# Row moments of the first layernorm taken on ScalarE with accumulators, in four of five pairs of tiles, in a graph-network kernel

## The chip, the cores and the metric

One core of one Trainium2 chip runs the whole program. The metric is device time in microseconds (us) of one execution; the times of a kernel are given as the median of several runs. Engines are named as the profile names them: PE is TensorE's matmuls and PEld its weight loads, DVE is VectorE, ACT is ScalarE, POOL is GpSimd, SP is SyncE; a q behind a name is that engine's DMA issuing.

## What is computed

Two graph networks in a row on 1250 nodes of 1024 features and 20000 edges. Only the head of the first one matters here:

```python
def layernorm(x, g, b):
    m = jnp.mean(x, axis=-1, keepdims=True)
    v = jnp.mean((x - m) ** 2, axis=-1, keepdims=True)
    return (x - m) * jax.lax.rsqrt(v + LN_EPS) * g + b

h = layernorm(x, ln_in_g, ln_in_b)          # x: 1250 x 1024
h = jax.nn.relu(h @ W1 + b1)                # 1024 -> 512
h = h @ W2 + b2                             # 512 -> 256
for i in range(3):                          # message passing, 20000 edges
    agg = jax.ops.segment_sum(h[src], dst, num_segments=n)
    ...
```

After it come a decoder back to 1024 features, two more layernorms, and two neighbourhood layers with 1024x1024 weights.

## The kernel before

The program has four stages, one after the other: `graph_block` (the first 168 us), the encoder, the decoder, and the two neighbourhood layers. The change touches only the first.

`graph_block` does two things at once. It turns the edge list into a dense matrix of edge counts (visits: VectorE builds two one-hot masks with `is_equal` at lines 410 and 411, PE multiplies them at line 586 into five banks), and it computes relu(layernorm(x) @ W1 + b1) (`dense`, line 622). The 1250 nodes are 10 tiles of 125 rows, taken as 5 pairs p = 0 to 4; the tiles of a pair are u = 0 and 1. A pair also has 5 groups j of 7 visits: six each at first, then the body of `more`, and one more each at the end.

Every engine's program is written out by hand and runs in that order; semaphores are the only link. For one pair the path of the layernorm is this. SP loads the rows into `x_rows[u]`, of which there are only two: the load of tile (p+1, u) may start once `normalize(p, u)` has read (p, u). VectorE's `statistics(p)` takes the moments with two `bn_stats` for each tile (line 386), two `bn_aggr` (394) and one add (396); ScalarE takes the root (`take_root`, 240); VectorE's `normalizer(p)` makes the reciprocal with a Newton step and the shift (63 to 71, 402). ScalarE's `normalize(p, u)` writes `xhat[u]` (248), PE turns it (`turn_norm(p, u)`, 579), ScalarE applies gain and bias and rounds (`affine(p, u)`, 257 and 262), VectorE keeps the rest (`norm_low`, 442), and PE can multiply.

On PE, the loop of pair p runs the four column blocks `dense(p-1, 0..3)` between the groups of counts of pair p; `turn_norm(p, 1)` stands behind `dense(p-1, 3)` and `turn_norm(p+1, 0)` at the loop's end. The turned rows go to banks that hold the products of `dense(p-1, 1)` and `dense(p-1, 2)`, so `turn_norm(p, 1)` also waits until ScalarE's `relu(p-1, 2)` (line 282) has read them, and `dense(p-1, 3)` waits for `relu(p-1, 0)`. VectorE writes its masks into a ring of 12 places and so can be two groups ahead of PE. ScalarE's other work is `read_counts` (274, ten copies out of the banks), `z1_high` (291) and the rounding of the weights (267).

In VectorE's program `statistics(1)` stands in pair 0 behind the visits of group 2; `statistics(p+2)` stands at the end of pair p, ahead of `z1_low(p-1)` and the visits of the next pair. `normalizer(p+1)` stands behind group 0 of pair p.

Of the kernel before, what the change touches and what calls it, by code (L numbers as in the profile page):

```python
# [5 lines left out]
ALU = mybir.AluOpType  # L6
ACT = mybir.ActivationFunctionType
AX = mybir.AxisListType
F32 = mybir.dt.float32
# [6 lines left out]
D, H, B, LAYERS = 1024, 512, 256, 3  # L16
NT = 125
# [3 lines left out]
PAIRS = T // 2  # L21
# [4 lines left out]
EPS = 1e-5  # L26
# [81 lines left out]
def graph_block(nc, block, sem, io, s):  # L108
# [20 lines left out]
    z1_mm, z1_relu, z1_hi, z1_split = sem("z1_mm"), sem("z1_relu"), sem("z1_hi"), sem("z1_split")  # L129
    at_stored, eye_added = [sem("at_stored0"), sem("at_stored1")], sem("eye_added")  # L130
    padded, places_set = sem("padded"), sem("places_set")

    at = Map(nc, s.work_at)
    w1 = at("w1", [128, 2, KD, H], F32R)
# [23 lines left out]
    var_eps, root, rstd, shift, scratch = [at(n, [128, 2], F32) for n in ("var_eps", "root", "rstd", "shift", "scratch")]  # L158
    trips_i = at("trips_i", [128, PAIRS], I32)
    iota = at("iota", [128, KEYS], F16)  # L160
    assert at.at <= nc.sbuf_usable_end, at.at - nc.sbuf_usable_end

    at = Map(nc, s.wide_at)
# [73 lines left out]
    def _(act):  # L237
        def take_root(p):
            act.wait_ge(var_ready, p + 1)
            act.activation(root[0:NT, :], var_eps[0:NT, :], ACT.Sqrt).then_inc(root_ready, 1)  # L240

        def normalize(p, u):
            t = 2 * p + u
            act.wait_ge(norm_ready, p + 1)
            act.wait_ge(x_in[u], 16 * (p + 1))
            if p > 0:
                act.wait_ge(xhat_read, t - 1)
            act.activation(xhat[u][0:NT, :], x_rows[u][0:NT, :], ACT.Identity, bias=shift[0:NT, u:u + 1],
                           scale=rstd[0:NT, u:u + 1]).then_inc(xhat_ready, 1)

# [54 lines left out]
        for n in range(2, KD // 2):  # L305
            w1_high(n)
        affine(0, 1)
        take_root(1)
        normalize(1, 0)
        normalize(1, 1)  # L310
        w1_high(KD // 2)
        for p in range(1, PAIRS):
            read_counts(p - 1)
            if p + 1 < PAIRS:
                take_root(p + 1)
            affine(p, 0)
            relu(p - 1, 0)
            relu(p - 1, 1)
            if p + 1 < PAIRS:
                normalize(p + 1, 0)  # L320
            relu(p - 1, 2)
            relu(p - 1, 3)
            z1_high(p - 1)
            affine(p, 1)
            if p + 1 < PAIRS:
                normalize(p + 1, 1)
# [55 lines left out]
    def _(dve):  # L382
# [2 lines left out]
            for h in range(2):  # L385
                dve.bn_stats(stats[0:NT, u, h, :], x_rows[u][0:NT, 512 * h:512 * h + 512]).then_inc(stat_step, 1)

        def statistics(p):
            if p > 0:
                row_sums(p, 0)  # L390
                row_sums(p, 1)
            dve.wait_ge(stat_step, 6 * p + 4)
            for u in range(2):
                dve.bn_aggr(mean_var[0:NT, u, :], stats[0:NT, u, :, :]).then_inc(stat_step, 1)
            dve.wait_ge(stat_step, 6 * p + 6)
            dve.tensor_scalar(var_eps[0:NT, :], mean_var[0:NT, :, 1], EPS, None, ALU.add).then_inc(var_ready, 1)

        def normalizer(p):
            dve.wait_ge(var_ready, p + 1)
            dve.wait_ge(root_ready, p + 1)  # L400
            newton_rstd(dve, norm_step, 5 * p, rstd[0:NT, :], var_eps[0:NT, :], root[0:NT, :], scratch[0:NT, :])
            dve.scalar_tensor_tensor(out=shift[0:NT, :], in0=mean_var[0:NT, :, 0], scalar=-1.0, in1=rstd[0:NT, :],
                                     op0=ALU.mult, op1=ALU.mult).then_inc(norm_ready, 1)

        def visit(n, g, v):

# [107 lines left out]
            dve.tensor_scalar(pick[0:EP, j, :], spread, table[0:EP, j:j + 1], None, ALU.is_equal).then_inc(picked, 1)  # L514
        dve.tensor_copy(visits[0:EP, :], spread.rearrange("p (g v) -> p g v", v=VISITS)[:, :, STATIC]).then_inc(row_step, 1)
        dve.tensor_copy(chunk_ids[0:EP, :], table[0:EP, 0:2]).then_inc(row_step, 1)
        statistics(0)
        w1_low(0)
        normalizer(0)
        dve.wait_ge(picks, 1)  # L520
# [7 lines left out]
        for p in range(PAIRS):  # L528
            for j in range(GROUP):
                for v in range(STATIC - 1):  # L530
                    visit(n, GROUP * p + j, v)
                    n += 1
                if p == 0:
                    if j == 1:
                        w1_low(1)
                        norm_low(0, 0)
                    if j == 2:
                        statistics(1)
                        w1_low(2)
                        w1_low(3)  # L540
                    if j == 3:
                        norm_low(0, 1)
                        normalizer(1)
                else:
                    if j == 0 and p + 1 < PAIRS:
                        normalizer(p + 1)
                    if j == 2:
                        norm_low(p, 0)
            if p == 0:
                dve.wait_ge(trips_known, PAIRS + 1)  # L550
            if p > 0:
                dve.wait_ge(hot_free, GROUP * STATIC * p + GROUP)
            last_trip = dve.value_load(trips_i[0:1, p:p + 1], min_val=p + 2, max_val=(C - STATIC) * (p + 1) + 1)
            more(p, first_trip, last_trip)
            first_trip = last_trip
            for j in range(GROUP):
                visit(n, GROUP * p + j, STATIC - 1)
                n += 1
            if p > 0:
                norm_low(p, 1)  # L560
            if p + 2 < PAIRS:
                statistics(p + 2)
            if p == 0:
                w1_low(KD // 2)
            else:
                z1_low(p - 1)
# [1342 lines left out]
```

## Time and profile before

| | us |
|---|---|
| median of 3 runs | 1071.99 |
| lowest, highest | 1071.13, 1073.99 |
| the profiled execution | 1074.08 |
| its span in the profile | 1072.3 |
| first stage, until PE's last `dense` | 168 |

So 1.8 us of the profiled execution lie outside its span, and it took 2.1 us more than the median. All starts of instructions below count from the start of the span. A profile row gives the start, the time (of all instructions of the row together, first start to last end), engine, line, operation, output and input, and in brackets the idle time ahead of it and what ended that idle time. Neighbouring rows overlap by some 0.1 us, because an instruction's end is drained while the next one starts; so the cost of a piece of a queue is best read as the distance between two starts.

### The profile page before, as it was taken

The numbers are of one execution on the slowest core, as the hardware profiler recorded it, in microseconds if no ns is written. First come the engines' busy times: TensorE is split into PE (matmuls) and PEld (weight loads), VectorE is DVE, ScalarE is ACT, GpSimd is POOL, SyncE is SP. The second block draws the span as 40 slices with busy tenths as digits, with TensorE's granted clock in tenths as the row PEclk, the third lists the DMA queues.
The fourth block names the chain that finished last, engine by engine and source line by source line (L and its number), as shares of the span: only waits on it lengthen the run. The fifth ranks groups of instructions, "written<-read, shape, count | busy, mean of one in ns | idle before, by whom it ended". The sixth has DMA issues, their size and how long they took to land.

```text
span 1072.3 us, 14807 instructions
## 1 busy us (share of the span) xinstructions
PE 1002.2 (93%) x4862; PEld 812.9 (76%) x4862; DVE 536.6 (50%) x1314; ACT 351.5 (33%) x632; POOL 263.8 (25%) x320
## 2 busy tenths in 40 slices
PE   4779899989897898999999999999999999999996
PEld 2367678878787687887777777778887777877774
DVE  7978974374658887333223332222234333334545
ACT  5545552152526477321111221113341011222221
POOL 3000003741416330735004324005206003300000
PEclk9698999999998999999999999999999999999999
DMA  9296344893003584414223104243325335103444
GB/s 327 67 220 186 49 64 89 195 204 84 2 20 109 188 281 150 144 32 138 100 100 102 45 20 160 67 141 128 108 87 166 120 97 164 46 1 121 154 133 133
DMA packets 48263, 127.13 MB, mean 119 GB/s; under 512 B 17775, under 2 KB 18784, under 8 KB 48016
## 3 DMA queue, kind: packets, MB, share of 16 engines
q1 hardware_dynamic: 33622, 74.91, 23.8%
q0 software_dynamic: 8288, 37.29, 12.9%
q10 hardware_dynamic: 6298, 14.21, 3.9%
q8 instruction: 33, 0.54, 0.2%
q14 instruction: 22, 0.18, 0.1%
HBM read 101.76 MB, written 45.13 MB: 137 GB/s over the span
## 4 chain that ended last, share of the span: by engine, by line
PE 83%; DVE 7%; ACT 3%; issue 3%; DMA 2%; POOL 1%; SPq 0%; ACTq 0%; DVEq 0%; POOLq 0%
PE bank L1724 42%; PE bank L1745 17%; PE bank L622 5%; PE bank L1071 5%; PE bank L1103 4%; PE bank L1431 4%; PE bank L586 3%; DMA x_rows<-x 1%; DVE wide L957 1%; PE bank L1412 1%; DVE wide L959 1%; PE bank L1445 1%; ACT xt_f L257 1%; DMA w_f<-W_pairs 1%; PE bank L579 0%
## 5 line engine op out<-in xcount | busy, mean ns | idle before, releaser
L1665 DVE TENSOR_TENSOR h_stage<-h_turned,h_stage 128x1000 fp32r<-128x1000 f32 x80 | 105.5, 1320 | 370.2 <-ACT h_stage L1597 370.2
L1724 PE MATMUL bank<-w_neigh,h_stage 128*125 128x512 f32 x960 | 227.2, 397 | 3.4 <-issue 3.4
L1724 PE MATMUL bank<-w_self,h_stage 128*125 128x512 f32 x960 | 230.3, 395 | 0.0
L1724 PEld LDWEIGHTS bank<-w_neigh,h_stage 128*125 128x125 f32 x960 | 178.2, 187 | 47.3 <-issue 3.6
L1724 PEld LDWEIGHTS bank<-w_self,h_stage 128*125 128x125 f32 x960 | 178.0, 186 | 45.6
L1745 PE MATMUL bank<-g_rows,a_stage 125*125 125x512 f32 x800 | 192.4, 395 | 0.0
L1597 ACT ACTIVATE h_stage<-h_turned 128x1000 fp32r (+1 forms) x80 | 83.8, 1049 | 305.9 <-PE bank L1724 293.5
L1745 PEld LDWEIGHTS bank<-g_rows,a_stage 125*125 125x125 f32 x800 | 148.4, 186 | 37.4
L1562 POOL CAST w_self<-w_stage 128x512 fp32r<-128x512 f32 x32 | 22.7, 711 | 230.2 <-PE bank L1724 221.9
L1103 PE MATMUL bank<-a_turned,gn 125*128 125x418 f32 x360 | 70.5, 354 | 2.8 <-DVE gn L963 2.8
L1103 PEld LDWEIGHTS bank<-a_turned,gn 125*128 125x128 f32 x360 | 67.0, 188 | 4.2 <-DVE gn L963 3.4
L622 PE MATMUL bank<-xt,w 128*128 128x252 f32 x480 | 65.0, 294 | 0.7 <-DVE xt L442 0.7
L622 PEld LDWEIGHTS bank<-xt,w 128*128 128x128 f32 x480 | 61.5, 197 | 2.7 <-DVE xt L442 1.0
L1431 PE MATMUL bank<-w_self,wide 128*125 128x512 f32 x240 | 58.5, 400 | 0.4 <-POOL w_self L844 0.4
L586 PE MATMUL bank<-hot_keys,hot_src 125*128 125x500 bf16 x155 | 45.4, 410 | 9.3 <-DVE hot_keys L411 8.6
L411 DVE TENSOR_SCALAR hot_keys<-iota,tab 125x500 bf16<-125x500 f16 x155 | 53.1, 343 | 0.0
L1431 PEld LDWEIGHTS bank<-w_self,wide 128*125 128x125 f32 x240 | 44.5, 189 | 11.4 <-POOL w_self L844 0.8
L1688 DVE SCALAR_TENSOR_TENSOR o<-bank,deg_inv,o 125x512 f32<-125x512 f32 x40 | 30.0, 751 | 36.8 <-PE bank L1745 34.7
L338 POOL TENSOR_TENSOR a_turned<-a_turned,ident 125x125 f32 x10 | 7.7, 789 | 149.0 <-DMA at_dram<-a_turned 149.0
L1564 POOL TENSOR_TENSOR w_self<-w_stage,w_self 128x512 fp32r<-128x512 f32 x32 | 43.3, 1354 | 2.6
L410 DVE TENSOR_SCALAR hot_src<-iota,tab 125x125 bf16<-125x125 f16 x155 | 40.8, 263 | 0.5 <-issue 0.4
L586 PEld LDWEIGHTS bank<-hot_keys,hot_src 125*128 125x128 bf16 x155 | 15.1, 101 | 34.0 <-DVE hot_keys L411 24.5
(210 smaller groups left out, 1125.6 us busy)
## 6 DMA issues: line engine op xcount, KB each, us to landing
a_stage<-at_dram SPq DMA_DIRECT2D x40, 625.0 KB, 4.1
w_stage<-w_self POOLq DMA_DIRECT2D x32, 256.0 KB, 3.2
at_dram<-a_turned SPq DMA_DIRECT2D x10, 625.0 KB, 10.5
w_stage<-w_neigh POOLq DMA_DIRECT2D x24, 256.0 KB, 2.9
dec_y<-x_bd SPq DMA_DIRECT2D x10, 512.0 KB, 4.0
dec_x<-x_ob SPq DMA_DIRECT2D x10, 512.0 KB, 4.8
x_dram<-h_rows SPq DMA_DIRECT2D x10, 512.0 KB, 3.0
h_dram<-o ACTq DMA_DIRECT2D x20, 256.0 KB
```

Of the source, the lines that this page charges most:

```text
L410: dve.tensor_scalar(place_src[0:EC, slot, 0:NT], iota[0:EC, 0:NT], tab[0:EC, 1, g, v:v + 1], None, ALU.is_equal)
L411: dve.tensor_scalar(place_keys[0:EC, slot, :], iota[0:EC, :], tab[0:EC, 0, g, v:v + 1], None, ALU.is_equal)\
L586: mm = pe.matmul(ps_counts[j][:, 0:KEYS], place_src[0:EC, slot, :], place_keys[0:EC, slot, :], start=start, stop=stop)
L622: mm = pe.matmul(ps_z1[m][:, 0:2 * NE], w1[:, a, k, m * 128:(m + 1) * 128], xt[:, own, b, k, :], start=(k == 0 and q == 0), stop=(k == KD ...
L1071: mm = pe.matmul(out, w(a, k), x(b, k), start=(k == 0 and p == 0), stop=(k == k_tiles - 1 and p == 2))
L1103: mm = pe.matmul(ps_z[j % 2][:, 0:CH], cast(gn[0:NT, h, k, m * 128:(m + 1) * 128]), cast(s.at_[0:NT, k, cols]), start=(k == 0 and h == 0), ...
L1431: mm = pe.matmul(y_banks[t % 2][c][0:NT, :], s.wide[:, a, k, t * NT:(t + 1) * NT], s.w_self[:, b, k * D + 512 * c:k * D + 512 * c + 512], ...
L1564: pool.tensor_tensor(lo, w_f32[u][:, :], raw(hi), ALU.subtract).then_inc(w_ready, 1)
L1597: act.activation(st[u][:, 0, :, :], ht[:, :, cols], ACT.Copy).then_inc(st_hi, 1)
L1665: dve.tensor_tensor(st[u][:, 1, :, :], ht[:, :, bass.ds(t * NT, NT)], raw(st[u][:, 0, :, :]), ALU.subtract).then_inc(st_ready, 1)
L1724: mm = pe.matmul(out, st[u][:, a, k, :], w[:, b, k * 512:(k + 1) * 512], start=(k == 0 and p == 0), stop=(k == KD - 1 and p == 2))
L1745: mm = pe.matmul(ps_a[u][0:NT, :], cast(a_st[u][0:NT, k, :]), cast(g[0:NT, h, k, :]), start=(k == 0 and h == 0), stop=(k == T - 1 and h == 1))
```

## The change

For the pairs 1 to 4 the moments move from VectorE to ScalarE. A new function `row_moments(p)` copies each tile with `accum_out` (the row's sum) and then takes Square with the bias minus the mean, again with `accum_out` (the sum of squared differences); both write their full output into `xhat[0]`, where nothing reads it. VectorE turns the sums into minus the mean (`means`) and the variance plus epsilon (`variances`). Pair 0 keeps `bn_stats`, with one small instruction more.

```diff
+        def row_moments(p):
+            act.wait_ge(xhat_read, 2 * p - 1)
+            for u in range(2):
+                act.wait_ge(x_in[u], 16 * (p + 1))
+                act.wait_ge(sums_ready, 2 * (p - 1) + u)
+                act.wait_ge(squares_ready, 2 * (p - 1))
+                act.activation(xhat[0][0:NT, :], x_rows[u][0:NT, :], ACT.Copy, accum_out=row_sum[0:NT, u:u + 1])\
+                   .then_inc(sums_ready, 1)
+            act.wait_ge(mean_ready, p)
+            for u in range(2):
+                act.wait_ge(sums_ready, 2 * p)
+                act.wait_ge(squares_ready, 2 * (p - 1) + u)
+                act.activation(xhat[0][0:NT, :], x_rows[u][0:NT, :], ACT.Square, bias=minus_mean[0:NT, u:u + 1],
+                               accum_out=row_squares[0:NT, u:u + 1]).then_inc(squares_ready, 1)
...
         affine(0, 1)
+        row_moments(1)
         take_root(1)
...
             read_counts(p - 1)
+            affine(p, 0)
             if p + 1 < PAIRS:
+                row_moments(p + 1)
                 take_root(p + 1)
-            affine(p, 0)
             relu(p - 1, 0)
...
+        def means(p):
+            dve.wait_ge(sums_ready, 2 * p)
+            dve.wait_ge(norm_ready, p)
+            dve.tensor_scalar(minus_mean[0:NT, :], row_sum[0:NT, :], -1.0 / D, None, ALU.mult).then_inc(mean_ready, 1)
+
+        def variances(p):
+            dve.wait_ge(squares_ready, 2 * p)
+            dve.wait_ge(norm_ready, p)
+            dve.tensor_scalar(var_eps[0:NT, :], row_squares[0:NT, :], 1.0 / D, EPS, ALU.mult, ALU.add).then_inc(var_ready, 1)
...
                     if j == 1:
                         w1_low(1)
                         norm_low(0, 0)
+                        means(1)
                     if j == 2:
-                        statistics(1)
                         w1_low(2)
                         w1_low(3)
+                        variances(1)
                     if j == 3:
                         norm_low(0, 1)
                         normalizer(1)
                 else:
-                    if j == 0 and p + 1 < PAIRS:
-                        normalizer(p + 1)
+                    if j == 1 and p + 1 < PAIRS:
+                        means(p + 1)
                     if j == 2:
                         norm_low(p, 0)
+                        if p + 1 < PAIRS:
+                            variances(p + 1)
+                    if j == 3 and p + 1 < PAIRS:
+                        normalizer(p + 1)
...
-            if p + 2 < PAIRS:
-                statistics(p + 2)
```

On ScalarE in the loop of pair 1, before, behind the counts of pair 0 (the last number of a row is the output's shape; z_f is the output of `relu`, wide that of `z1_high`):

```order
L240 ACTIVATE root<-var_eps 125x2
L257 ACTIVATE xt_f_77<-bank,ln_gb 128x125 x8
L262 ACTIVATE xt<-xt_f_77 128x8x125
L282 ACTIVATE z_f_80<-bank,biases 128x252 x2
L248 ACTIVATE xhat_86<-x_rows_84,shift,rstd 125x1024
```

and now (the lines of the changed kernel have other numbers):

```order
L276 ACTIVATE xt_f_77<-bank,ln_gb 128x125 x8
L281 ACTIVATE xt<-xt_f_77 128x8x125
L251 ACTIVATE xhat_86,row_sum<-x_rows_84 125x1024
L251 ACTIVATE xhat_86,row_sum<-x_rows_85 125x1024
L257 ACTIVATE xhat_86,row_squares<-x_rows_84,minus_mean 125x1024
L257 ACTIVATE xhat_86,row_squares<-x_rows_85,minus_mean 125x1024
L242 ACTIVATE root<-var_eps 125x2
L301 ACTIVATE z_f_80<-bank,biases 128x252 x2
L267 ACTIVATE xhat_86<-x_rows_84,shift,rstd 125x1024
```

The affine step now comes ahead of the root, and four passes over rows stand between it and the first two `relu`.

On VectorE in pair 0, around the visits of group 2 (one of its six pairs of masks is shown at each end), before:

```order
L442 TENSOR_TENSOR xt<-xt_f_77,xt 128x8x125
L410 TENSOR_SCALAR hot_src<-iota,tab 125x125
L411 TENSOR_SCALAR hot_keys<-iota,tab 125x500
...
L386 BN_STATS stats<-x_rows_84 125x6 x2
L386 BN_STATS stats<-x_rows_85 125x6 x2
L394 BN_AGGR mean_var<-stats 125x2 x2
L396 TENSOR_SCALAR var_eps<-mean_var 125x2
L455 TENSOR_TENSOR w_75<-w_f_2_107,w_75 128x1024
```

and now:

```order
L474 TENSOR_TENSOR xt<-xt_f_77,xt 128x8x125
L420 TENSOR_SCALAR minus_mean<-row_sum 125x2
L442 TENSOR_SCALAR hot_src<-iota,tab 125x125
L443 TENSOR_SCALAR hot_keys<-iota,tab 125x500
...
L487 TENSOR_TENSOR w_75<-w_f_2_110,w_75 128x1024
L487 TENSOR_TENSOR w_75<-w_f_3_111,w_75 128x1024
L425 TENSOR_SCALAR var_eps<-row_squares 125x2
```

The statistics are gone from behind the visits, and an instruction that needs ScalarE's sums stands ahead of them.

## Rows read from the trace of the kernel before

**Rows 1.** Page, part 1: busy time of PE, share of the span.

```profile
PE 1002.2 (93%) x4862; PEld 812.9 (76%) x4862; DVE 536.6 (50%) x1314; ACT 351.5 (33%) x632; POOL 263.8 (25%) x320
```

**Rows 2.** Windows of pairs: length, busy PE, PEld, DVE, ACT, POOL, granted clock, DMA.

```profile
71.00:104.00 33.00, 26.58 (x165) 20.27 (x165) 25.64 (x102) 16.07 (x40) 2.36 (x4) 0.84 0.77 201
104.00:133.00 29.00, 25.88 (x167) 19.52 (x166) 25.88 (x103) 16.34 (x41) 2.22 (x2) 0.94 0.40 63
133.00:156.00 23.00, 22.54 (x152) 17.04 (x152) 20.71 (x88) 13.31 (x34) 1.38 (x2) 1.00 0.44 57
```

**Rows 3.** Timeline of PE: the four second turns, and the counts behind idle time.

```profile
63.92 1.02 PE L579 MATMUL bank<-ident,xhat 125*128 125x125 f32 x8
...
81.36 2.24 PE L586 MATMUL bank<-more_keys,more_src 125*128 125x500 bf16 x5 [6.29 <-DVE more_keys L411]
...
96.50 1.02 PE L579 MATMUL bank<-ident,xhat 125*128 125x125 f32 x8
...
110.56 2.20 PE L586 MATMUL bank<-more_keys,more_src 125*128 125x500 bf16 x5 [2.96 <-DVE more_keys L411]
...
124.82 1.02 PE L579 MATMUL bank<-ident,xhat 125*128 125x125 f32 x8
...
148.20 1.02 PE L579 MATMUL bank<-ident,xhat 125*128 125x125 f32 x8
```

**Rows 4.** Timeline of DVE: the two waits in statistics(3) and statistics(4).

```profile
77.81 1.29 DVE L386 BATCH_NORM_STATS2 stats<-x_rows 125x6 f32<-125x512 f32 x2 [4.75 <-DMA x_rows<-x]
...
107.02 1.29 DVE L386 BATCH_NORM_STATS2 stats<-x_rows 125x6 f32<-125x512 f32 x2 [1.38 <-DMA x_rows<-x]
```

**Rows 5.** Timeline of DVE in pair 0, from norm_low(0, 0) to group 4.

```profile
24.32 1.20 DVE L442 TENSOR_TENSOR xt<-xt_f,xt 128x1000 fp32r<-128x1000 f32 x1 [0.52 <-ACT xt L262]
...
27.97 2.46 DVE L386 BATCH_NORM_STATS2 stats<-x_rows 125x6 f32<-125x512 f32 x4
...
30.86 2.35 DVE L455 TENSOR_TENSOR w<-w_f,w 128x1024 fp32r<-128x1024 f32 x2
33.13 0.25 DVE L410 TENSOR_SCALAR hot_src<-iota,tab 125x125 bf16<-125x125 f16 x1
...
35.67 1.20 DVE L442 TENSOR_TENSOR xt<-xt_f,xt 128x1000 fp32r<-128x1000 f32 x1
...
37.84 0.25 DVE L410 TENSOR_SCALAR hot_src<-iota,tab 125x125 bf16<-125x125 f16 x1
```

**Rows 6.** Timeline of ACT: a plain copy, a square with accumulator, its readout.

```profile
24.19 1.99 ACT L267 ACTIVATE w<-w_f 128x1024 fp32r<-128x1024 f32 x2
...
357.74 1.15 ACT L1301 ACTIVATE squares<-dec_y,dec_minus_mean 125x1024 bf16<-125x1024 f32 x1 [4.52 <-DVE dec_minus_mean L1374]
358.79 0.19 ACT L1301 ACTIVATION_READ_ACCUMULATOR squares<-dec_y,dec_minus_mean 125x1 f32 x1
```

**Rows 7.** Timeline of ACT: pair 0, then pairs 3 and 4.

```profile
28.98 1.04 ACT L262 ACTIVATE xt<-xt_f 128x1000 fp32r<-128x1000 f32 x1
...
46.13 2.97 ACT L274 ACTIVATE a_turned<-bank  x10 [4.85 <-PE bank L586]
...
125.02 0.47 ACT L282 ACTIVATE z_f<-bank,biases 128x252 f32<-128x252 f32 x1 [3.67 <-PE bank L622]
...
131.53 2.77 ACT L274 ACTIVATE a_turned<-bank  x10
134.12 2.95 ACT L257 ACTIVATE xt_f<-bank,ln_gb 128x125 f32<-128x125 f32 x8
...
138.05 0.45 ACT L282 ACTIVATE z_f<-bank,biases 128x252 f32<-128x252 f32 x1
```

**Rows 8.** Line 220, row loads issued at 70.7, then 90.1: issue to landing.

```profile
DMA to landing us min/median/max: 7.0/7.0/7.0
...
DMA to landing us min/median/max: 13.1/13.1/13.1
```

**Rows 9.** Timeline of POOL: the first of the copies issued beside the loads.

```profile
63.22 0.51 POOL L374 DMA_DIRECT2D x_bd<-x  x1
```

More of the change, by code:

```diff
@@ L131, in graph_block @@
     padded, places_set = sem("padded"), sem("places_set")
+    sums_ready, mean_ready, squares_ready = sem("row_sums_ready"), sem("row_mean_ready"), sem("row_squares_ready")
     at = Map(nc, s.work_at)
@@ L160, in graph_block @@
     iota = at("iota", [128, KEYS], F16)
+    row_sum, row_squares, minus_mean = [at(n, [128, 2], F32) for n in ("row_sum", "row_squares", "minus_mean")]
     assert at.at <= nc.sbuf_usable_end, at.at - nc.sbuf_usable_end
@@ L247, in normalize @@
                 act.wait_ge(xhat_read, t - 1)
+                act.wait_ge(squares_ready, 2 * p)
             act.activation(xhat[u][0:NT, :], x_rows[u][0:NT, :], ACT.Identity, bias=shift[0:NT, u:u + 1],
@@ L386, in row_sums, with statistics @@
                 dve.bn_stats(stats[0:NT, u, h, :], x_rows[u][0:NT, 512 * h:512 * h + 512]).then_inc(stat_step, 1)
[L388 to L392, printed above, removed]
+        def statistics():
+            dve.wait_ge(stat_step, 4)
             for u in range(2):
                 dve.bn_aggr(mean_var[0:NT, u, :], stats[0:NT, u, :, :]).then_inc(stat_step, 1)
-            dve.wait_ge(stat_step, 6 * p + 6)
+            dve.wait_ge(stat_step, 6)
+            dve.tensor_scalar(minus_mean[0:NT, :], mean_var[0:NT, :, 0], -1.0, None, ALU.mult).then_inc(stat_step, 1)
             dve.tensor_scalar(var_eps[0:NT, :], mean_var[0:NT, :, 1], EPS, None, ALU.add).then_inc(var_ready, 1)
+        def means(p):
[6 more added lines that the diff above has]
+            dve.tensor_scalar(var_eps[0:NT, :], row_squares[0:NT, :], 1.0 / D, EPS, ALU.mult, ALU.add).then_inc(var_ready, 1)
         def normalizer(p):
@@ L401, in normalizer @@
             newton_rstd(dve, norm_step, 5 * p, rstd[0:NT, :], var_eps[0:NT, :], root[0:NT, :], scratch[0:NT, :])
-            dve.scalar_tensor_tensor(out=shift[0:NT, :], in0=mean_var[0:NT, :, 0], scalar=-1.0, in1=rstd[0:NT, :],
-                                     op0=ALU.mult, op1=ALU.mult).then_inc(norm_ready, 1)
+            if p == 0:
+                dve.wait_ge(stat_step, 7)
+            else:
+                dve.wait_ge(mean_ready, p)
+            dve.tensor_tensor(shift[0:NT, :], minus_mean[0:NT, :], rstd[0:NT, :], ALU.mult).then_inc(norm_ready, 1)
         def visit(n, g, v):
@@ L516, in _ @@
         dve.tensor_copy(chunk_ids[0:EP, :], table[0:EP, 0:2]).then_inc(row_step, 1)
-        statistics(0)
+        statistics()
         w1_low(0)
```

## The prediction, made before the changed kernel ran

> **What bounds the kernel now.** I read first the page's busy shares: PE is busy 93% of the span [rows 1], so a gain can only come from where PE stands still. The change is in the first stage, so I cut that stage into its pairs with the windows. PE is busy 26.6 of 33 us in pair 2, 25.9 of 29 in pair 3, 22.5 of 23 in pair 4, and its granted clock is 0.84, 0.94 and 1.00 of full speed [rows 2]: pairs 2 and 3 lose time twice, by waiting and by the lower of the two clock levels behind the wait. The timeline of PE gives the same as a period. From one `turn_norm(p, 1)` to the next it takes 96.50 - 63.92 = 32.6 us, then 28.3, then 23.4; PE stood idle 6.29 and 2.96 us in the first two, both times for VectorE's masks [rows 3]. The timeline of DVE tells why the masks were late: `statistics(3)` and `statistics(4)` stand ahead of them in VectorE's queue and waited 4.75 and 1.38 us for the second tile's rows [rows 4]. That wait, behind the statistics' own time of 27.97 to 30.86 = 2.9 us a pair [rows 5], is what the change takes away from VectorE. Behind the first stage nothing is edited, and PE runs into the encoder without a break, so I let a gain or loss at 168 us pass through unchanged.
>
> **Pair 0: what the change costs.** Here PE waits for masks and VectorE is the bound. The new `means(1)` stands on VectorE directly behind `norm_low(0, 0)`, which frees the queue at about 25.4 [rows 5]. It needs ScalarE's sums, and ScalarE only reaches them behind `affine(0, 1)`, whose last instruction starts at 28.98 and lasts 1.0 [rows 7]. One sum is a copy of 1024 columns, 1.0 us by the distance in a pair of copies (1.99 for two), plus the readout of the accumulator, 0.19 us [rows 6], plus a few hundredths for the wait on the sum before: 1.25. So the sums are there at 30.1 + 2.5 = 32.6 (0.1 for the extra small instruction of pair 0), and the mean at 32.8. VectorE stands still from 25.4 to 32.6, and its six visits of group 2, the next groups and PE's counts are all queued behind. Then: six visits, 33.13 to 35.67 = 2.5 [rows 5], to 35.3; two weight roundings 30.86 to 33.13 = 2.3, to 37.6; `variances(1)` 0.2, to 37.8 (the squares are done at 35.4, hidden); six visits, to 40.3. Before, that point was 35.67 [rows 5]. **Pair 0 ends 4.7 us later**, although 2.9 us of statistics are gone.
>
> **Pair 1: the new ring.** `read_counts(0)` starts when PE has the last count of pair 0, at 46.13 + 4.7 = 50.8 [rows 7]. From there the parts hang on each other across three engines: 2.8 for the counts (all but the last overlap of that row's 2.97), `affine(1, 0)` 134.12 to 138.05 = 3.9 [rows 7], two sums 2.5, `means(2)` 0.25 with its handoff; then on VectorE six visits 2.5, `norm_low` 1.1, `variances` 0.2, six visits 2.5, `normalizer(2)` 1.1 (with `norm_low`, 35.67 to 37.84 is 2.2) [rows 5] and 0.1 of handoff, 7.5 together; on ScalarE `normalize(2, 0)` and `relu(0, 2)`, 1.65. Sum: 50.8 + 2.8 + 3.9 + 2.5 + 0.25 + 7.5 + 1.65 = 69.4, and only then may PE start `turn_norm(1, 1)`, because `relu(0, 2)` stands behind `normalize(2, 0)`, and that behind the normalizer, which was moved from group 0 to group 3. Before it started at 63.92 [rows 3]: **5.5 us late**. PE itself would be there 1.7 us earlier. Removed `statistics(2)` buys nothing here; it only fills part of VectorE's wait for the sums. The two squares (2.6) lie beside VectorE's visits and `norm_low` (3.6), so they cost nothing until they are 1 us dearer.
>
> **Pairs 2 and 3: what it brings.** The same ring closes on itself. From `relu(p-1, 3)` to the end of `affine(p+1, 0)` ScalarE's queue needs 125.02 to 138.05 = 13.0 us, counts included [rows 7]; then 2.5 + 0.25 + 7.5 + 1.65 as above: 24.9, and with a few handoffs of hundredths **25.1 us a pair**. PE alone needs 23.4 (pair 4, [rows 3]), so PE now waits 1.7 us a pair, in front of the turn. Against 32.6 and 28.3 that is 7.5 and 3.2 us gained; the lost clock is in these numbers, since waits of 1.7 us instead of 6.29 and 2.96 should leave it alone, and if they don't, slower products fall into the same wait. Pair 4 has no moments and stays at 23.4.
>
> **The row loads, moved past.** `row_moments` itself waits for the rows. A tile (p+1, 1) is asked for when `normalize(p, 1)` ends, and `sum` of it starts 131.53 to 134.12 = 2.6, plus 3.9, plus 1.25 = 7.8 us later [rows 7]. The nearest row is the load issued at 70.7, in the same place of the loop, beside the large copies that POOL issues from 63.22 on: 7.0 us [rows 8, 9]. It would just be hidden. But the normalizer's move also brings the load of tile (p+1, 0) to within 8 us of it and on top of those copies, where the load issued at 90.1 took 13.1 us [rows 8]; its 0.5 MB will share the engines. Bounds for the second load are so 7.0 and 13.1, which is 0 to 5.3 us of ScalarE's waiting in each of two pairs. I take 8.1, near the first since it comes equally late in the copies: 0.3 a pair, 0.7 in all with rounding up.
>
> **The sum.** +5.5 - 7.5 - 3.2 + 0.7 = -4.5 us. On the profiled execution that is 1074.08 - 4.5 = 1069.6; that execution took 2.1 us more than the median, and I forecast the median: 1071.99 - 4.5 = **1067.5**. A sum pass may cost between 1.0 (readout free) and 1.35 (as dear as the square with its readout and a wait); eight such passes lie on the path, so -2.0 to +0.8.
>
> The rules for kernel authors in the Trainium skill, "ScalarE: Activation LUTs", speak against the change: adds and multiplies belong on VectorE, which is faster per element. The trace agrees on the busy time: 5.1 us on ScalarE in place of 2.9 on VectorE. By that rule alone, with both on the path, the four pairs would lose 4 x 2.2 = 8.8 us; what speaks against it is that the squares lie beside VectorE's work. The same page's pricing, 186 ns plus 0.833 ns a column for an ACTIVATE without pointer operands, would make the copy 1.04 us, as the row has it.
>
> **Rivals.**
> *The loads take the place of the statistics' wait (slower).* If both second loads take 13.1 us, ScalarE waits 5.3 us in each of two pairs with `relu`, root and normalize queued behind it, and PE behind those: +5.5 - 10.7 + 10.6 = +5.4, 1077.4. It is slower than the bound of 0.3% from a landing of 12.0 us on. For: loads, copies and the counts' stores meet in one stretch, and one load did take 13.1. Against: that one was issued just behind the copies, the second tile's is issued 7 us later. Chance 0.11.
> *Late, but less.* Landings of 8.5 to 12, or a start that is dearer by 1 to 2 us: the gain shrinks to within 3.2 us of nothing, 1069 to 1075. Chance 0.27.
> *PE stays the bound.* If the ring closes faster than PE's 23.4 us, because handoffs and passes are cheap and VectorE's visits run ahead, it is +5.5 - 9.2 - 4.9 = -8.6, 1063.4. For: my ring is only 1.7 us longer than PE's period. Against: ten rows would all have to be too long. Chance 0.09.
> *All extra ScalarE time is on the path*, one mechanism: the squares outlast VectorE's cover because VectorE is idle behind them. Then 4 x 2.2 more than now, 1080. It is the case that the skill's rule, above, gives. Chance 0.03.
>
> **How the numbers follow.** My forecast holds with 0.50, at 1064.5 to 1068.7; there faster. A measurement of this kernel can tell about 0.3%, or 3.2 us, from no change. Faster: 0.50 + 0.09, rounded to 0.59; within: 0.27; slower: 0.11 + 0.03 = 0.14. The range 1064.0 to 1073.0 takes in the cheap passes at one end and one late load of 13.1 us at the other, and leaves out most of the slower cases and half of the PE-bound one.
>
> **What the profile of the changed kernel would show.** VectorE idle for 7 us at 25 us, ended by ScalarE's sums; `turn_norm(1, 1)` at 69.4; turns 25 us apart in the next two pairs, each behind a wait of 1.5 to 2 us for ScalarE; no PE wait for masks over 1 us after 50 us; last `dense` ending 4 to 5 us before 168. The forecast is wrong if ScalarE's sums wait for rows by more than 2 us, if the clock stays low behind pair 1, or if the sum with its readout lasts over 1.5 us.

## The result and the profile after

The changed kernel takes 1067.84 us (median of 14 runs, 1065.48 to 1070.97) against 1071.19 us (14 runs, 1068.97 to 1074.49) for the kernel before. The medians lie 3.35 us apart, which is a ratio of 0.9969; the ratio on record is 0.996 with a 95% interval of 0.9947 to 0.9974, that is 2.8 to 5.7 us faster. 1067.5 was forecast. Its profiled execution took 1067.81 us, its span is 1066.0 us, 6.3 us shorter than that of before. One later run of the kernel before (1656 us) and two of the variant h1 below (1427 and 3544 us) were in a slow state and are left out of all medians and ratios.

The timeline of PE in the changed kernel, the four second turns and the first product of the encoder (columns: start, us, engine, line, operation; in brackets the idle time ahead and what ended it). It answers to [rows 3]:

```profile
69.80 1.05 PE L614 MATMUL bank<-ident,xhat 125*128 125x125 f32 x8 [1.16 <-ACT z_f L301]
...
94.87 1.04 PE L614 MATMUL bank<-ident,xhat 125*128 125x125 f32 x8 [1.51 <-ACT z_f L301]
...
120.06 1.04 PE L614 MATMUL bank<-ident,xhat 125*128 125x125 f32 x8 [1.72 <-ACT z_f L301]
...
143.45 1.02 PE L614 MATMUL bank<-ident,xhat 125*128 125x125 f32 x8
...
162.86 13.87 PE L1106 MATMUL bank<-wide,weight_slots 128*128 128x418 f32 x72
```

The first turn is 5.9 us later than before, then the turns are 25.1, 25.2 and 23.4 us apart in place of 32.6, 28.3 and 23.4. The large waits for masks are gone; in their place stands a wait of 1.2 to 1.7 us for z_f, which is `relu(p-1, 2)`. The encoder's first product started at 167.98 before and starts at 162.86 now, so **the first stage gives 5.1 us**. The remaining 1.2 us of the spans' difference come from behind it, where nothing was changed.

The same stretches as windows of the changed kernel (length, busy PE, PEld, DVE, ACT and POOL with counts, granted clock, DMA share, GB/s), which answer to [rows 2]:

```profile
69.80:94.87 25.07, 23.44 (x161) 18.12 (x161) 22.36 (x98) 20.37 (x46) 2.14 (x4) 1.00 0.88 231
94.87:120.06 25.19, 23.36 (x160) 18.03 (x161) 22.41 (x98) 20.36 (x46) 1.02 (x2) 1.00 0.75 195
120.06:143.45 23.39, 23.27 (x160) 18.12 (x161) 22.19 (x93) 14.32 (x35) 1.02 (x2) 1.00 0.39 55
```

PE is busy for nearly all of each, and in these three windows its clock stays at the full level where the kernel before had 0.84 and 0.94. In pair 0 it does not: behind the waits for masks both kernels have the lower level (0.50), before until about 46 us and now until about 53, and `turn_norm(1, 0)` takes 1.87 us in place of 1.02. ScalarE is busy 20 of 25 us, so it is now close to a bound of its own.

VectorE in pair 0 of the changed kernel, which answers to [rows 5]:

```profile
24.29 1.20 DVE L474 TENSOR_TENSOR xt<-xt_f,xt 128x1000 fp32r<-128x1000 f32 x1 [0.52 <-ACT xt L281]
32.29 0.17 DVE L420 TENSOR_SCALAR minus_mean<-row_sum 125x2 f32<-125x2 f32 x1 [6.80 <-ACT xhat L251]
...
39.78 1.19 DVE L474 TENSOR_TENSOR xt<-xt_f,xt 128x1000 fp32r<-128x1000 f32 x1
```

and ScalarE beside it, which answers to [rows 6, 7]:

```profile
28.95 1.04 ACT L281 ACTIVATE xt<-xt_f 128x1000 fp32r<-128x1000 f32 x1
29.90 1.04 ACT L251 ACTIVATE xhat<-x_rows 125x1024 f32<-125x1024 f32 x1
30.84 0.19 ACT L251 ACTIVATION_READ_ACCUMULATOR xhat<-x_rows 125x1 f32 x1
31.11 1.06 ACT L251 ACTIVATE xhat<-x_rows 125x1024 f32<-125x1024 f32 x1
```

VectorE stands still for 6.80 us for ScalarE's sums, and the second `norm_low` comes at 39.78 instead of 35.67. A sum with its readout takes 31.11 - 29.90 = 1.21 us.

### The profile page after: what moved, and what is told of

The parts are those of the page before. It is cut to its first block, busy times and chain, and to the rows that moved or that the text cites. A ratio compares the mean times of both kernels' runs of the same rounds, so it can differ in the third digit from the quotient of the medians.

```text
span 1066.0 us, 14861 instructions
## 1 busy us (share of the span) xinstructions
PE 998.9 (94%) x4862; PEld 811.5 (76%) x4862; DVE 522.4 (49%) x1295; ACT 370.3 (35%) x664; POOL 263.3 (25%) x320
## 4 chain that ended last, share of the span: by engine, by line
PE 80%; DVE 7%; issue 2%; ACT 2%; POOL 1%; ACTq 0%; DVEq 0%; POOLq 0%
PE bank L1759 42%; PE bank L1780 17%; PE bank L1106 5%; PE bank L1138 4%; PE bank L1466 4%; PE bank L657 3%; PE bank L621 2%; PE bank L1447 1%; PE bank L1480 1%; DVE wide L992 1%; DVE wide L994 1%; DVE hot_keys L443 1%; DVE hot_src L442 1%; POOL h_f L843 0%; PE bank L1165 0%
## 5 line engine op out<-in xcount | busy, mean ns | idle before, releaser
L657 PE MATMUL bank<-xt,w 128*128 128x252 f32 x480 | 62.4, 287 | 0.7 <-DVE xt L474 0.7
L657 PEld LDWEIGHTS bank<-xt,w 128*128 128x128 f32 x480 | 59.0, 190 | 3.0 <-DVE xt L474 1.0
L621 PE MATMUL bank<-hot_keys,hot_src 125*128 125x500 bf16 x155 | 46.0, 420 | 12.7 <-DVE hot_keys L443 12.2
L621 PEld LDWEIGHTS bank<-hot_keys,hot_src 125*128 125x128 bf16 x155 | 15.2, 102 | 37.1 <-DVE hot_keys L443 27.3
L1646 ACT ACTIVATE o<-o 125x512 f32<-125x512 f32 x20 | 12.6, 632 | 83.1 <-DVE o L1723 83.1
```

What stands on the lines that cost most here:

```text
L621: mm = pe.matmul(ps_counts[j][:, 0:KEYS], place_src[0:EC, slot, :], place_keys[0:EC, slot, :], start=start, stop=stop)
L657: mm = pe.matmul(ps_z1[m][:, 0:2 * NE], w1[:, a, k, m * 128:(m + 1) * 128], xt[:, own, b, k, :], start=(k == 0 and q == 0), stop=(k == KD ...
```

## The experiments

Twelve kernels ran in three groups of four; each group was on one chip with its own runs of the kernel before, so times are compared as ratios to those. The ratio on record is not the quotient of the two medians beside it and differs from it by up to 0.0015; a difference of less than some 2 us between two kernels is therefore not told from none. All edits start from the changed kernel unless it says otherwise. "Turns" are the starts of `turn_norm(p, 1)`, "encoder" the first product behind the first stage, both from each kernel's one profile.

| kernel | median us | before us | ratio (95%) | turns | encoder |
|---|---|---|---|---|---|
| before | | | 1 | 63.9, 96.5, 124.8, 148.2 | 168.0 |
| changed | 1067.84 | 1071.19 | 0.996 (0.9947-0.9974) | 69.8, 94.9, 120.1, 143.5 | 162.9 |
| e1 means late | 1066.59 | 1073.73 | 0.9935 (0.9916-0.9955) | 62.9, 88.2, 115.5, 138.9 | 158.3 |
| e2 relu first | 1071.72 | 1073.73 | 0.9977 (0.9965-0.9989) | 68.2, 96.5, 120.9, 146.4 | 165.8 |
| e3 pair 1 on VectorE | 1068.01 | 1073.73 | 0.9945 (0.9927-0.9964) | 66.4, 91.9, 117.7, 141.1 | 160.5 |
| e4 statistics moved | 1071.21 | 1073.73 | 0.9978 (0.9959-0.9996) | 64.6, 91.2, 119.3, 144.3 | 164.1 |
| f1 changed, again | 1070.42 | 1073.16 | 0.9965 (0.995-0.9981) | 72.0, 97.2, 122.6, 147.6 | 167.1 |
| f2 e1 + copies late | 1063.77 | 1073.16 | 0.9913 (0.9897-0.9928) | 62.8, 89.4, 114.6, 138.0 | 157.4 |
| f3 normalizer sooner | 1068.14 | 1073.16 | 0.996 (0.9945-0.9975) | 67.7, 92.5, 117.0, 142.7 | 162.1 |
| f4 all three | 1063.64 | 1073.16 | 0.9905 (0.9889-0.9921) | 61.1, 87.0, 111.6, 137.3 | 156.7 |
| h1 VectorE only | 1064.70 | 1071.34 | 0.9938 (0.9915-0.996) | 63.2, 87.5, 113.3, 137.9 | 157.6 |
| h2 before, copies late | 1068.42 | 1071.34 | 0.9962 (0.9941-0.9982) | 64.4, 92.3, 121.3, 144.7 | 166.0 |
| h3 changed, copies late | 1068.03 | 1071.34 | 0.9966 (0.9946-0.9986) | 70.1, 95.3, 120.7, 145.7 | 165.1 |
| h4 sums twice | 1080.23 | 1071.34 | 1.0068 (1.0043-1.0093) | 75.3, 104.5, 132.1, 155.5 | 174.9 |

The theory under test is that of the prediction: VectorE's wait for ScalarE's sums costs pair 0 some 4.7 us, and from there a ring of links over three engines sets the period. The rivals are that VectorE's saved work is the gain, that the wait for rows is, or that ScalarE has room.

**e1: the wait in pair 0 taken out.**

```diff
                     if j == 1:
                         w1_low(1)
                         norm_low(0, 0)
-                        means(1)
                     if j == 2:
                         w1_low(2)
                         w1_low(3)
-                        variances(1)
                     if j == 3:
+                        means(1)
                         norm_low(0, 1)
-                        normalizer(1)
+                    if j == 4:
+                        variances(1)
...
             more(p, first_trip, last_trip)
             first_trip = last_trip
+            if p == 0:
+                normalizer(1)
```

> The changed kernel, but in pair 0 VectorE takes means(1) behind group 3, variances(1) behind group 4 and normalizer(1) behind the extra trip, so that it no longer stands still for ScalarE's sums. Theory (the 4.7 us by which pair 0 ends later come from VectorE's 6.8 us wait at 25.5 us): the wait is gone, turn_norm(1, 1) comes 5 us sooner than in the changed kernel, at about 64.8 instead of 69.8, and all behind it too; the last dense ends near 157.9, the time is 5 us below the changed kernel's. Rival (the wait only fills time that PE or ScalarE lose in pair 0 anyway): turn_norm(1, 1) stays within 1 us of 69.8.

The first turn comes at 62.9, 6.9 us sooner than in the changed kernel, and the encoder 4.5 us sooner. So pair 0's price is real and can be avoided. In time 5 us were expected against the changed kernel; by the ratios it is 2.7 to 3.2 (0.9935 against 0.996 and 0.9965, on other chips). Part of the 6.9 us is lost again in the later periods, because something else came up. The timeline of ScalarE in e1:

```profile
77.79 1.06 ACT L251 ACTIVATE xhat<-x_rows 125x1024 f32<-125x1024 f32 x1 [0.65 <-DMA x_rows<-x]
...
102.76 1.06 ACT L251 ACTIVATE xhat<-x_rows 125x1024 f32<-125x1024 f32 x1 [1.20 <-DMA x_rows<-x]
...
104.95 1.06 ACT L251 ACTIVATE xhat<-x_rows 125x1024 f32<-125x1024 f32 x1 [1.04 <-DMA x_rows<-x]
```

These are sums that wait for rows, the prediction's slower rival, and the third period is 27.3 us. The four loads took 13.5, 8.5, 14.9 and 10.3 us to land.

**e2: the last link ahead of the turn taken out.**

```diff
             relu(p - 1, 1)
+            relu(p - 1, 2)
             if p + 1 < PAIRS:
                 normalize(p + 1, 0)
-            relu(p - 1, 2)
             relu(p - 1, 3)
```

> The changed kernel with relu(p-1, 2) ahead of normalize(p+1, 0) on ScalarE. Theory (PE's wait before the turn is only where the ring sums, VectorE's visits, normalizer, normalize, z1_high, affine, counts, affine, sums shows; the relu is one link of 0.4 us in it): PE's wait in front of turn_norm(p, 1) goes, but it comes back in front of the extra trip's counts or of dense(p, 3); the turns stay 24.5 to 24.9 us apart (25.1 before), the time is 1 to 2 us below the changed kernel's. Rival (the order of relu and normalize is the whole wait): the turns come 23.4 us apart, the waits of 1.2, 1.5 and 1.7 us vanish, and the time falls by 4.4 us.

PE's waits in front of the turns are gone, yet the periods are 28.3, 24.4 and 25.5 us and the time did not fall: 0.9977 against 0.9965 for the changed kernel on another chip. The rival, that the order of the two is the whole wait, is out. The second period, 24.4, is close to the 24.5 to 24.9 of the theory; the first holds 1.63 and 0.81 us of sums waiting for rows and a stretch of low clock behind a wait for `relu(1, 0)`, where 24 matmuls took 4.63 us instead of 3.1:

```profile
92.00 4.63 PE L657 MATMUL bank<-xt,w 128*128 128x252 f32 x24 [1.40 <-ACT z_f L301]
```

The last period has low clock too (0.93). The 1 to 2 us that I expected of it did not show.

**e3: pair 1 back on VectorE.** The edit takes `row_moments(1)`, `means(1)` and `variances(1)` out and puts the four `bn_stats` and their sequel back behind group 2 of pair 0:

```diff
         affine(0, 1)
-        row_moments(1)
...
                         norm_low(0, 0)
-                        means(1)
                     if j == 2:
+                        row_sums(1, 0)
+                        row_sums(1, 1)
+                        statistics(1)
                         w1_low(2)
                         w1_low(3)
-                        variances(1)
```

> The changed kernel with the moments of pair 1 back on VectorE, at their old place in pair 0; pairs 2 to 4 stay on ScalarE. Theory: pair 0 is that of the kernel before, turn_norm(1, 1) starts at about 65.2 (4.6 us sooner than in the changed kernel, 1.3 us later than before it), the later periods stay 25.1, 25.2 and 23.4; the time is 4.6 us below the changed kernel's. Rival (pair 1's new ring, not pair 0, costs the start): turn_norm(1, 1) stays at 68 or later.

The first turn is at 66.4, 3.4 us sooner than in the changed kernel and 2.5 later than before, where 1.3 was expected; this execution's PE began pair 1 1.7 us later than that of before (first turn of the pair at 48.55 against 46.89). The encoder is 2.3 us sooner than in the changed kernel, and by the ratios the time 1.6 to 2.1 us less, where 4.6 were expected. So most of the late start is pair 0's, as e1 shows too, and some 1 to 2 us of it may be the new ring already in pair 1; the later beginning of this execution cannot be told from that. One load waited 0.53, another 1.15 us.

**e4: the order of the change without ScalarE's passes.** From the kernel before:

```diff
             read_counts(p - 1)
+            affine(p, 0)
             if p + 1 < PAIRS:
                 take_root(p + 1)
-            affine(p, 0)
...
                 else:
-                    if j == 0 and p + 1 < PAIRS:
-                        normalizer(p + 1)
+                    if j == 1 and p + 1 < PAIRS:
+                        statistics(p + 1)
                     if j == 2:
                         norm_low(p, 0)
+                    if j == 3 and p + 1 < PAIRS:
+                        normalizer(p + 1)
...
             if p > 0:
                 norm_low(p, 1)
-            if p + 2 < PAIRS:
-                statistics(p + 2)
```

> The kernel before with bn_stats kept on VectorE for all pairs, but statistics(p+1) moved from the end of pair p-1 to behind group 1 of pair p, normalizer(p+1) to behind group 3, and affine(p, 0) ahead of the root: the order of the change without its ScalarE passes. Theory (what the change gains is that VectorE no longer waits for the rows ahead of the masks, not that VectorE has 2.9 us a pair less to do): PE's waits of 6.29 and 2.96 us for masks are gone, turn_norm(1, 1) is at 63.9 to 65.3, the turns then come 25.5 to 25.9 us apart, the last dense ends about 3.5 us sooner than in the changed kernel and 8 to 9 us sooner than before. Rival (the work taken from VectorE is the gain): the periods stay above 28 us, and the time within 3 us of the kernel before.

The large waits for masks are gone here too, with all of `bn_stats` still on VectorE, so it is the place of the statistics in VectorE's queue that held PE up. But the periods are 26.6, 28.1 and 25.1 instead of 25.5 to 25.9 and 23.4, and the time is only 2.5 us below before (0.9978). The windows between the turns say where it went:

```profile
64.57:91.19 26.62, 23.42 (x161) 18.09 (x161) 25.23 (x103) 15.67 (x38) 1.93 (x5) 1.00 0.87 218
91.19:119.25 28.06, 25.03 (x160) 18.47 (x161) 25.33 (x104) 16.04 (x38) 1.72 (x4) 0.94 0.81 206
119.25:144.32 25.07, 24.94 (x161) 18.69 (x162) 22.17 (x96) 14.78 (x35) 0.18 (x1) 0.93 0.42 52
```

The first of these, at full clock, is 26.6 us and ends in a wait of PE of 3.07 us; a wait of 2.91 us ends the second. Behind each of the two the granted clock falls (0.94 and 0.93 over the period), and PE is busy 25 us for work of 23.4. The rival forecast two things. Its time came true (within 3 us of before), its periods only in the second case (28.1), where the low clock makes them. But VectorE's 2.9 us do count. In this kernel the ring runs through other links than in the changed one: from PE's turn at 64.57 to the extra visit's table on VectorE at 69.04, through VectorE's queue to the end of the normalizer at 89.4, in which VectorE waited only 0.37 us, and over `normalize` and `relu` to the turn at 91.19. The statistics are a link of it. VectorE is busy 25.2 of its 26.6 us.

**f1: the changed kernel again.**

> The changed kernel once more, unedited, so that it stands on the same chip as the next three. Theory: turns at about 70, 95, 120 and 143.5 us, a second tile's load (issued at about 76 and 101) that lands 6.8 to 7.5 us later and so just in time for its sum; time 3 to 5 us below the kernel before. Rival (the landing is not stable from run to run): the second tile's sums wait for rows by 0.5 to 3 us and the middle periods are 26 us and more.

The ratio is nearly the same as at first, 0.9965. The loads' rival did not come: the second tiles landed in 6.8 and 6.3 us. But this profiled execution took 1075.47 us, and it shows two things that the first did not. Its weights arrived later at the very start (ScalarE's first product of them at 13.37 instead of 12.18, and a second wait of 0.86 us for them), so VectorE waited 7.8 instead of 6.8 us for the sums and the first turn was at 72.0. And the clock fell behind the last of the three waits:

```profile
97.23:122.56 25.33, 23.35 (x160) 18.04 (x161) 22.53 (x98) 20.41 (x46) 1.30 (x2) 1.00 0.76 194
122.56:147.63 25.07, 24.95 (x161) 18.81 (x161) 22.18 (x93) 14.85 (x35) 1.06 (x2) 0.93 0.36 52
```

PE's 23.4 us of work took 25.1, and in this last period, which no ring lengthens, all 1.7 us count.

**f2: e1 and POOL's copies away from the loads.**

```diff
-            own = slice(p * CH, min((p + 1) * CH, N + 128 - NT))
-            for to in ("x_bd", "x_ob") if p < NCH else ():
+            part_no = {0: 0, 3: 1, 4: 2}.get(p, NCH)
+            own = slice(part_no * CH, min((part_no + 1) * CH, N + 128 - NT))
+            for to in ("x_bd", "x_ob") if part_no < NCH else ():
```

> The kernel with the late means in pair 0 (the first experiment), and POOL issues the second and third part of its x copies in pairs 3 and 4 in place of 1 and 2, away from the row loads. Theory (the row loads landed 8.5 to 14.9 us after issue there because they share the DMA engines with these copies, and ScalarE waited 2.9 us for them): loads land in 3.6 to 5 us, no sum waits for rows, the turns are 25.1 us apart instead of 25.4 and 27.3, and the last dense ends 2 to 3 us sooner than at 158.3. Rival (the loads are late for another reason, such as the stores of the counts): landings stay at 8 us and over and the periods at 25.4 and 27.3.

All four loads landed in 3.4 to 3.8 us, no sum waits for rows, and the ratio is 0.9913. The second period is the ring's 25.1. The encoder comes only 0.9 us sooner than in e1, where 2 to 3 us were expected, since the first period is 26.7 us: it had low clock behind a wait of 1.84 us (the turn of 1.02 us took 1.78). The timeline of PE, and that of ScalarE some us later:

```profile
62.75 1.78 PE L617 MATMUL bank<-ident,xhat 125*128 125x125 f32 x8 [1.84 <-ACT z_f L301]
...
70.29 3.54 ACT L293 ACTIVATE a_turned<-bank  x10 [0.65 <-PE bank L624]
```

ScalarE, which waits for PE neither here nor at its affine step in the changed kernel's first period, now waits 0.65 and 0.43 us. So a fall of the clock directly behind the turn is not absorbed by the ring; it makes the ring itself longer, by 1.6 us here. By the ratio the time is 2.4 us better than e1's, with intervals that touch.

**f3: one link out of the ring.**

```diff
                         if p + 1 < PAIRS:
                             variances(p + 1)
-                    if j == 3 and p + 1 < PAIRS:
-                        normalizer(p + 1)
+                            normalizer(p + 1)
```

> The changed kernel with normalizer(p+1) directly behind variances(p+1) in the pairs 1 to 3, ahead of group 3's visits instead of behind them. Theory (the ring of 25.1 us is a sum of links; this one takes 2.5 us of visits out of it and puts 0.3 us of waiting for the root in): PE's waits of 1.2, 1.5 and 1.7 us in front of the turns go, a wait of 0.7 to 1 us for masks comes up elsewhere, the periods are 23.6 to 24.2 us, the last dense ends 3 us sooner than at 162.9. Rival (VectorE's visits are what PE waits for, so their delay costs what the sooner normalizer gains): periods stay at 25. The loads rival: ScalarE arrives sooner at the sums and waits for rows, 1 to 2 us a pair, which gives half of it back.

No turn waits any more, and the periods are 24.7, 24.5 and 25.7 where 23.6 to 24.2 were expected: shorter than 25.1, but by less. PE now waits twice a pair for VectorE's extra visit, 0.4 to 0.7 us each time and 1.1 to 1.2 together, and in the last period the clock was at 0.93. The encoder comes at 162.1, 0.8 us before the changed kernel's and not 3. No sum waited for rows, so the loads' rival did not come. In time it is 2.3 us below f1 on the same chip (1068.14 against 1070.42), but the intervals of the two ratios overlap.

**f4: the three edits of e1, f2 and f3 together.**

> The changed kernel with all three edits: late means in pair 0, POOL's copies in pairs 3 and 4, normalizer directly behind variances. Theory: the effects add up, since each takes away another link: turn_norm(1, 1) near 61.5, periods 23.6 to 24.2, last dense ends near 151.5, 11 us before the changed kernel's 162.9; time 11 us below it, 14 to 15 us below the kernel before. Rival (they shadow each other): less than 8 us below the changed kernel.

It is the fastest, 0.9905, 6.8 us below f1 on the same chip and 9.5 below before. But 11 was expected of it against the changed kernel, and it is level with f2: the rival (the edits shadow each other, less than 8 us) is right. The turns are 25.9, 24.5 and 25.7 us apart. The timeline of PE:

```profile
65.46 0.57 PE L631 MATMUL bank<-more_pick,edge_keys 80*125 80x5 f32 x4 [0.57 <-DVE more_pick L454]
...
67.06 1.94 PE L643 MATMUL bank<-more_keys,more_src 125*128 125x500 bf16 x5 [0.60 <-DVE more_keys L462]
```

Two short waits for VectorE, then five matmuls take 1.94 us that take 1.23 elsewhere: the low clock again, and once more at 120 us (0.93 in the first and the last period). In this one profile the clock takes back what the sooner normalizer gains.

**h1: no ScalarE passes at all.** From e4, with `normalizer(p+1)` directly behind `norm_low(p, 0)` and f2's copies.

> The kernel before, with bn_stats on VectorE for all pairs, statistics(p+1) behind group 1 of pair p and normalizer(p+1) directly behind norm_low(p, 0) of group 2, affine(p, 0) ahead of the root, and POOL's copies in pairs 3 and 4. It has the order of the best version so far but none of ScalarE's passes, and pair 0 as before. Theory (order and loads are what matters, not which engine takes the moments): no PE wait for rows, periods of 24 to 25 us, last dense at 156 to 158, time within 2 us of the 1063.7 of the versions with ScalarE's passes. Rival (VectorE's 2.9 us a pair come back as late masks): periods of 26 us and more, time 4 us or more above 1063.7.

The periods are 24.4, 25.8 (with the clock at 0.93) and 24.5, the encoder starts at 157.6, within 1 us of f2 and f4: that part is as the theory has it. The ratio 0.9938 is worse than theirs, by 2.7 and 3.5 us, but the intervals touch, and it was another chip. So the order and the loads give most of the gain on either engine; whether ScalarE's passes add 2 or 3 us stays open. They do change one thing: here VectorE is busy 74.0 of the 74.7 us of the three periods and is the bound, against 67 of 75 in f2. With the statistics on it, VectorE has no room left.

**h2: the loads alone.** The kernel before with f2's copies and nothing else.

> The kernel before with nothing but POOL's copies moved to pairs 3 and 4. Theory (of VectorE's two waits in the statistics, 4.75 and 1.38 us, the landing is one part and the place in the queue the other): the second tile's load lands in 3.6 us instead of 7.0, VectorE waits 1.4 us twice, PE's wait of 6.29 falls to about 3 us, the first period from 32.6 to 28 to 29 us; time 3.5 to 5 us below the kernel before. Rival (landing does not depend on the copies in this kernel): no change.

```profile
78.51 2.24 PE L587 MATMUL bank<-more_keys,more_src 125*128 125x500 bf16 x5 [2.93 <-DVE more_keys L412]
...
106.18 2.24 PE L587 MATMUL bank<-more_keys,more_src 125*128 125x500 bf16 x5 [2.77 <-DVE more_keys L412]
```

PE's wait of 6.29 us fell to 2.93, VectorE's in the statistics from 4.75 and 1.38 to 1.38 and 1.17. The first period is 27.9 us, the second 29.0 and not shorter than before, with the clock at 0.88. The ratio is 0.9962: three changed lines in POOL's program are worth as much as the change. What is left of PE's wait, 2.9 us, has the size of the statistics' own time; that it is theirs was not tested in this kernel.

**h3: the changed kernel with f2's copies.**

> The changed kernel with nothing but POOL's copies moved to pairs 3 and 4. Theory (in the changed kernel the rows land just in time for their sums): no wait is there to take away, periods 25.1 to 25.3, time within 1.5 us of the changed kernel, 3 to 4 us below the kernel before. Rival (the copies also delay it, in executions that no profile showed): 3 us or more below the changed kernel, about 7 us below the kernel before.

Loads in 3.5 to 3.6 us, periods of 25.3, 25.3 and 25.1, ratio 0.9966: no change, and ScalarE waits for rows neither here nor in the changed kernel's profile. Here too the clock fell in the last period (0.93), behind a wait of 1.86 us.

**h4: the suspected cost doubled.**

```diff
+    sums_again = sem("row_sums_again")
...
+                act.activation(xhat[0][0:NT, :], x_rows[u][0:NT, :], ACT.Copy, accum_out=row_sum[0:NT, u:u + 1])\
+                   .then_inc(sums_again, 1)
+                act.wait_ge(sums_again, 2 * (p - 1) + u + 1)
                 act.activation(xhat[0][0:NT, :], x_rows[u][0:NT, :], ACT.Copy, accum_out=row_sum[0:NT, u:u + 1])\
                    .then_inc(sums_ready, 1)
```

> The changed kernel with each sum pass taken twice, two more passes of 1.25 us in each of the pairs 1 to 4, the second overwriting the first's result. Theory (ScalarE's sums are links of the ring and of pair 0's start): pair 0 ends 2.5 us later, turn_norm(1, 1) 5 us later than in the changed kernel, at about 75, the next two periods 27.6 to 27.8 us, the last 23.4; in all 10 us slower than the changed kernel. Rival (ScalarE, busy a third of the span, has room for them): less than 3 us slower.

The first turn is at 75.3 (75 was expected), the periods are 29.2, 27.7 and 23.4 us:

```profile
75.25:104.47 29.22, 25.65 (x160) 18.41 (x161) 22.52 (x97) 23.02 (x50) 2.13 (x4) 0.94 0.77 198
104.47:132.13 27.66, 25.50 (x161) 19.50 (x161) 22.63 (x98) 22.67 (x50) 1.36 (x2) 0.94 0.63 147
132.13:155.52 23.39, 23.27 (x161) 18.12 (x162) 22.20 (x93) 14.32 (x35) 1.31 (x2) 1.00 0.37 55
```

The ratio is 1.0068, which against 0.996 to 0.9966 for the changed kernel is 11 to 12 us for 10 us of added passes; by the medians it is 12.2 above h3 on the same chip. An engine that is busy a third of the span has no room at all at this place. Low clock behind the first turn (8.8 us instead of 7.1 to the next pair's first turn) explains what the first period has above 27.7. In the second period the clock fell at 127 us, ahead of the turn, and that fall did disappear in PE's wait, which is 0.33 instead of 2 us.

## Why the prediction was right, and where it was not

- **Pair 0.** 4.7 us were forecast. VectorE's idle time ended at 32.29 (32.6 forecast), the second `norm_low` is 4.1 us late, and ScalarE's counts start at 50.57 (50.8), 4.4 late. e1 shows that this price is real, and h4 that it follows ScalarE's sums (VectorE waits 9.16 us for them there).
- **Pair 1.** The first turn was forecast for 69.4 and came at 69.80: 5.9 late instead of 5.5. PE's own wait there was 1.16 and not 1.7 us: its clock was still at the lower level when pair 1 began, and `turn_norm(1, 0)` alone took 0.85 us more.
- **The ring.** 25.1 us were forecast; 25.07 and 25.19 were measured, 25.25 and 25.33 in f1. A sum costs 1.21 us, not 1.25. e2, f3 and h4 tell the ring from its rivals: taking the last link away moves the wait, taking an inner link away shortens the period by 0.6 us (less than forecast, since other waits come up), and adding 2.5 us to a link lengthens it by 2.5.
- **The loads.** The first tiles landed late, as argued: 12.0 and 12.8 us. For the second tiles I took 8.1 us; it was 6.8 and 7.5 [rows 8 for before], under the 7.8 of cover. So the term was 0 instead of 0.7. The forecast chance of a late landing was not idle: with the order of e1, e2 and e3 it did happen, at 0.5 to 1.6 us a time.
- **The sum.** In the two profiles the first stage is 5.9 - 7.5 - 3.1 = 4.7 us shorter at the fourth turn, and 5.1 at the encoder. My sum without the loads was 5.2. The median moved by 3.35. That leaves 1.7 us, but 5.1 lies inside the interval of the ratio (2.8 to 5.7 us), so this gap may be nothing. That the forecast of 1067.5 was met within 0.34 us is in part luck: I started 0.8 us too high (1071.99 from three runs, 1071.19 from fourteen) and forecast 1.15 us too much gain.
- **The clock.** I had expected waits of 1.7 us to leave the clock at its full level, and slower products, if there were any, to fall into the same wait. **That step was wrong:** two of the three profiles with the changed order (f1, h3) show the low clock in pair 4, where it costs 1.7 us of the period in full, and f2 shows that directly behind the turn it lengthens the ring; only the profile that came with the result has neither. Such a fall would have the size of the gap above; that the median contains it is argued from these profiles, not shown. Also, the time from the encoder on, where nothing differs in the program, is 902.5 to 907.4 us in the fourteen profiles, so 1 or 2 us of a single pair of profiles mean nothing.
- **A slip.** The case of all extra ScalarE time on the path comes to 1071.99 + 8.8 = 1080.8, not 1080. It changes no chance.
- **The rule that speaks against the change**, adds and multiplies on VectorE (the Trainium skill, "ScalarE: Activation LUTs", the rules for kernel authors), would by my estimate have made it 8.8 us slower with everything on the path. The squares stayed hidden: VectorE's `variances` followed group 2's visits and `norm_low` without a wait. h1 gives the rule some right all the same: with a good order VectorE alone reaches the same first stage within 1 us. The Trainium skill's price for an ACTIVATE without pointer operands ("ScalarE: Activation LUTs", "What ACT_TABLE_LOAD costs") gives 1.04 us for a copy of 1024 columns; the rows of the sums agree, 1.04 and 1.06, with the readout on top.

## What to carry to other kernels

A wait for a transfer costs most where it stands in an in-order queue ahead of work that others need; moving the waiting step behind that work, or moving the transfers that crowd the load, can be had without moving the computation to another engine. Where three engines hand work round in a loop, add up the links between two turns of it: an engine that is busy a third of the time can still be on that ring, and then each of its microseconds counts. When an early result is moved to another engine, look at the first iteration by itself: that the consumer asks for it before the producer can have it cost here more than half of what the later iterations gained.

## What the runs showed of the hardware that I had not expected

- The granted clock fell behind short waits of PE, and not always, and the length of the wait does not tell when. It fell behind a wait of 1.40 us (e2), 1.66 (h4), 1.84 (f2) and 1.86 (f1, h3), and behind two waits of 0.57 and 0.60 us with eight small matmuls between (f4). It did not behind 1.72 us in the changed kernel, 1.76 and 2.01 in e1 or 2.02 in h4, nor behind the same two short waits one pair later in f4. With one such fall in a period PE is busy 24.6 to 25.1 us for work that takes 23.3 to 23.4, so it costs 1.2 to 1.8 us. What makes it fall was not tested.
- A load of 0.5 MB took up to 14.9 us to land beside POOL's copies of 1.7 MB (e1) and 3.4 to 3.8 us once these were issued in later pairs (f2, f4, h1, h3). It depends on the moment: with the copies in their old place, loads of f3 landed in 3.6, 7.6, 3.4 and 8.2 us. The copies' place was worth 3 to 4 us of the kernel before (h2).
- The first weights arrived at 12.18 us after the start in one execution of the changed kernel and at 13.37 in another (f1), and the first turn was at 69.80 and 71.98. The 1.2 us grew to 2.2; that the changed kernel suffers more from it than the one before, because VectorE waits for ScalarE in pair 0, is argued and not shown.
